# The second layer's output projection as three half-precision products, with VectorE writing the low half of the turned y

## What is computed

```python
    y = jnp.einsum('bhqk,bkhd->bqhd', att, v)
    y = y.reshape(Bx, Tx, HD)
    return y @ w_out
...
x = x + _L1_attn_ref(xn, w_kv_down, w_kv_up, w_q, w_out) + _L1_ffn_ref(xn, ...)
```

## Time and profile before

| | |
|---|---|
| median of 3 runs | 2831.82 us |
| the profiled execution: its own time, its span | 2835.03 us, 2833.2 us |
| PE, matmul busy | 2749.2 us, 97% of the span, 28612 instructions |
| DVE busy | 2341.8 us, 83%, 4378 instructions |
| ACT busy | 2078.8 us, 73% |
| POOL (GpSimd) busy | 1556.0 us, 55% |
| mean granted TensorE clock | 0.994 of full speed |

### The profile page before, as it was taken

How to read it: one execution, slowest core, us unless ns; L and a number is a source line. 1 busy time by engine, 2 the same in 40 slices (tenths; PEclk the granted TensorE clock), 3 DMA queues, 4 the chain that set the end, 5 groups by cost and what they waited for, 6 DMA issues and landing times.

```text
span 2833.2 us, 74040 instructions
## 1 busy us (share of the span) xinstructions
PE 2749.2 (97%) x28612; PEld 1665.3 (59%) x28612; DVE 2341.8 (83%) x4378; ACT 2078.8 (73%) x4411; POOL 1556.0 (55%) x1360
## 2 busy tenths in 40 slices
PE   5999999999999997999999999999999999999999
PEld 3656666666556553655665655656556656655665
DVE  6888888888888768988888888888888888888886
ACT  3777777777777776777777777777767767767766
POOL 2333343343333334766666666657656666666665
PEclk8999999999999998999999999999999999999999
DMA  4222222222222225344353444444444443443442
GB/s 136 58 57 68 75 65 64 58 64 64 57 58 68 69 71 158 95 113 110 86 128 96 99 119 107 99 109 114 102 109 105 102 114 91 110 118 84 108 119 52
DMA packets 249052, 260.52 MB, mean 92 GB/s; under 512 B 28288, under 2 KB 228992, under 8 KB 248448
## 3 DMA queue, kind: packets, MB, share of 16 engines
q1 hardware_dynamic: 226000, 239.70, 33.5%
q10 hardware_dynamic: 22704, 16.09, 1.9%
HBM read 107.84 MB, written 21.50 MB: 46 GB/s over the span
## 4 chain that ended last, share of the span: by engine, by line
PE 54%; DVE 5%; SPq 1%; issue 1%; DMA 1%; ACT 0%; DVEq 0%
PE l_ps_any L1584 7%; PE l_ps_any L1585 7%; PE l_ps_any L1586 7%; PE l_ps_any L1720 6%; PE l_ps_exp L1679 4%; PE l_ps_exp L1681 4%; PE l_ps_any L1729 4%; PE l_ps_any L1578 3%; PE l_ps_any L1654 3%; PE l_ps_out L1701 2%; PE l_ps_out L1704 2%; DVE l_neg_max L1512 2%; PE l_ps_out L1702 2%; PE l_ps_exp L1683 2%; SPq L1221 1%; DVE l_hw L1542 1%
## 5 line engine op out<-in xcount | busy, mean ns | idle before, releaser
L1278 POOL TENSOR_TENSOR stage<-l_p_in,stage 128x512 f16<-128x512 f32 x640 | 768.3, 1216 | 360.7 <-ACT l_p_in L1389 360.7
L725 DVE TENSOR_REDUCE neg_max<-ps_any 128x1 f32<-128x384 f32 (+3 forms) x704 | 407.1, 636 | 96.4 <-PE ps_any L854 92.8
L1287 POOL TENSOR_TENSOR l_hid<-l_hid,l_spread 128x512 f32<-128x512 f32 x256 | 347.6, 1358 | 215.8 <-DVE l_hid L1538 150.2
L1385 ACT ACTIVATE stage<-l_ps_exp 128x512 f16<-128x512 f32 x640 | 386.3, 604 | 91.5 <-PE l_ps_exp L1683 85.2
L477 POOL TENSOR_SCALAR_AFFINE_SELECT probs<-probs 128x512 f32<-128x512 f32 x256 | 162.1, 648 | 454.6 <-ACT probs L569 406.1
L569 ACT ACTIVATE probs<-ps_exp 128x512 f32<-128x512 f32 x640 | 348.3, 600 | 65.1 <-PE ps_exp L869 60.4
L1389 ACT ACTIVATE l_p_in<-l_ps_exp 128x512 f32<-128x512 f32 x640 | 388.7, 607 | 0.0
L1512 DVE TENSOR_REDUCE l_neg_max<-l_ps_any 128x2 f32<-128x768 f32 (+2 forms) x384 | 314.3, 859 | 16.0 <-PE l_ps_any L1659 15.8
L1679 PE MATMUL l_ps_exp<-l_q_a,l_k_a 128*128 128x512 f16 (+3 forms) x1024 | 303.4, 299 | 1.0 <-DMA l_q_b<-l_max_row 1.0
L1681 PE MATMUL l_ps_exp<-l_q_b,l_k_b 66*128 66x512 f16 (+3 forms) x1024 | 295.5, 300 | 0.0
L1542 DVE TENSOR_TENSOR l_hw<-l_hid,l_hw 128x512 f16<-128x512 f32 x272 | 260.6, 958 | 36.9 <-ACT l_hw L1367 36.5
(11 more groups left out here) (270 smaller groups left out, 7282.5 us busy)
## 6 DMA issues: line engine op xcount, KB each, us to landing
l_spread<-route_scratch SPq DMA_DIRECT2D x128, 512.0 KB, 4.4
l_q_a<-l_q_hi SPq DMA_DIRECT2D x256, 128.0 KB, 2.4
l_q_b<-l_q_lo SPq DMA_DIRECT2D x128, 128.0 KB, 2.4
l_k_a<-l_k_hi SPq DMA_DIRECT2D x128, 128.0 KB, 2.4
l_k_a<-l_k_lo SPq DMA_DIRECT2D x128, 128.0 KB, 2.4
l_k_b<-l_k_hi SPq DMA_DIRECT2D x128, 128.0 KB, 2.5
q_st<-rot_hi SPq DMA_DIRECT2D x64, 128.0 KB
k_st<-rot_hi SPq DMA_DIRECT2D x64, 128.0 KB
```

The lines of the kernel that those rows point to most:

```text
L725: nc.vector.tensor_reduce(neg_max[:, n % 2, heads[0]:heads[0] + k, t], src, AX.X, ALU.max, negate=True).then_inc(drained["dve"], 1)
L1278: nc.gpsimd.tensor_tensor(probs[:, n % 2, 1, u], p_in[:, m % P_SLOTS], probs[:, n % 2, 0, u], ALU.subtract).then_inc(p_lo_ok.sem, 1)
L1287: nc.gpsimd.tensor_tensor(at, at, spread[:, c % 3, n % SPREAD], ALU.mult).then_inc(weighted.sem, 1)
L1385: nc.scalar.activation(probs[:, n % 2, 0, u], bank, ACT.Exp, scale=float(HD1) ** -0.5).then_inc(exp_done.sem, 1)
```

## The change

`out` becomes three f16 products of halves. `yT` holds two halves in f16 in the same bytes. ACT writes the high half, without scale; DVE writes the low half with `low_part`, and it is now DVE's read that empties the bank of `turn_y`. `w_out` is loaded to `acc`'s space and halved once, with `w_d`. The scale is taken out when `out` is added to `acc`, in one instruction as before.

```diff
-        w_out = sb("w_out", [P, PAIRS, D])
+        w_out = sb("w_out", [P, 2, PAIRS, D], F16)
...
-        yT = sb("yT", [P, PAIRS, T])
+        yT = sb("yT", [P, PAIRS, 2, T], F16)
...
+        w_out_in = acc[:].rearrange("p s (k d) -> p (s k) d", d=D)
...
-        banks = Banks(program, filled_by1, filled_by1, lambda step: step[0] in ("gate", "cT", "turn_max", "turn_y"))
+        banks = Banks(program, filled_by1, filled_by1, lambda step: step[0] in ("gate", "cT", "turn_max"))
...
-        late_loads.append([(w_out[:], a["L1_attn_w_out"].rearrange("(k p) d -> p k d", p=P))])
+        late_loads.append([(w_out_in, a["L1_attn_w_out"].rearrange("(k p) d -> p k d", p=P))])
...
-        split_late = [(w_u, w_u_in), (w_d, w_d_in)]
+        split_late = [(w_u, w_u_in), (w_d, w_d_in), (w_out, w_out_in)]
...
                     act.wait_ge(down_loaded, 32)
+                    act.wait_ge(out_loaded, 16)
                     high_weights(split_late[1:])
...
-                    nc.scalar.activation(yT[:, n], bank, ACT.Copy, scale=1.0 / V_SCALE).then_inc(drained["act"], 1)
+                    nc.scalar.activation(yT[:, n, 0], bank, ACT.Copy).then_inc(y_hi_ok.sem, 1)
...
+                if name == "turn_y":
+                    if b and n % SET == 0:
+                        filling(dve, f"out{b - 1}_{n // SET}")
+                    low_part(f"turn_y{b}_{n}", yT[:, n, 1], yT[:, n, 0], 1.0, y_hi_ok, y_hi_ok.at(PAIRS * b + n, 1))
...
-                    nc.vector.tensor_tensor(acc[:, b % 2], full(dve, f"out{b}_{n}"), acc[:, b % 2], ALU.add
-                                            ).then_inc(drained["dve"], 1)
+                    nc.vector.scalar_tensor_tensor(out=acc[:, b % 2], in0=full(dve, f"out{b}_{n}"),
+                                                   scalar=1.0 / (W_SCALE * V_SCALE), in1=acc[:, b % 2], op0=ALU.mult,
+                                                   op1=ALU.add).then_inc(drained["dve"], 1)
...
                     for p in range(SET * n, SET * n + SET):
-                        ins = pe.matmul(out, w_out[:, p], yT[:, p], start=(p == SET * n), stop=(p == SET * n + SET - 1))
+                        for cw, cy in ((0, 0), (0, 1), (1, 0)):
+                            ins = pe.matmul(out, w_out[:, cw, p], yT[:, p, cy], start=(p == SET * n and cw + cy == 0),
+                                            stop=(p == SET * n + SET - 1 and cw == 1))
```

More of the change, by code:

```diff
@@ L1129, in layer1 @@
         w_u_in = experts_of_all(hw[:].rearrange("p s c t -> p (s c t)").bitcast(F32))
-        w_d_in = experts_of_all(yT[:].rearrange("p n t -> p (n t)"))
+        w_d_in = experts_of_all(yT[:].rearrange("p n c t -> p (n c t)").bitcast(F32))
+        w_out_in = acc[:].rearrange("p s (k d) -> p (s k) d", d=D)
         program = layer1_program(batches)
-        banks = Banks(program, filled_by1, filled_by1, lambda step: step[0] in ("gate", "cT", "turn_max", "turn_y"))
+        banks = Banks(program, filled_by1, filled_by1, lambda step: step[0] in ("gate", "cT", "turn_max"))
         up_loaded, down_loaded, out_loaded, weights_hi, weights_lo, prep, prep_pool = [
@@ L1165, in layer1 @@
         weighted = sig("weighted", 1)
+        y_hi_ok = sig("y_hi_ok", 1)
         hw_hi = sig("hw_hi", 1)
@@ L1724, in _ @@
                     if b == 0:
-                        pe.wait_ge(out_loaded, 16)
+                        pe.wait_ge(weights_lo, len(split_in) + len(split_late))
                     emptied(pe, f"turn_y{b}_{SET * n + SET - 1}")
```

## The result

| | before | after |
|---|---|---|
| median | 2831.39 us (4 runs, 2828.69 to 2832.66) | 2891.41 us (4 runs, 2890.30 to 2893.79) |
| the profiled execution: its own time, its span | 2835.03, 2833.2 us | 2892.00, 2889.9 us |

The ratio is 1.021, with a 95% interval of 1.0198 to 1.0222: 60 us slower. The forecast was 37 us slower, 2868.5 in 2843 to 2890. The side was right; the size was not, and the time lies just past the range. The clock (0.993) is as before.

The account below looks back on a forecast made before the run. PE's stream sets the pace, but only a few fills ahead of DVE's bank emptying; places 36.6 us, halving `w_out` +1.2, tail -1.1 gave +36.7 on 2835.03: 2871.7, less 3.2 for the median, 2868.5, range 2843 to 2890.

Parts of the forecast that it names:

- the leads at the banks: Second layer: an added 0.60 us DVE pass costs what PE's lead at that bank lacks; busy shares don't decide.
- PE's part: At a turn's two `out` steps, f16 products save 0.85 and 0.94 us; after waits 0.04 and 0.03 remain.
- `turn_y` 0, 1, 4, 7: Low halves there, per turn: 0 costs 0.53 us, 1 nothing; 4 and 7 leave gains of 0.04 and 0.03.
- `turn_y` 2: Low half there makes PE stand 1.23 us for its bank; part comes back, 0.5 a turn taken.
- `turn_y` 5 and 6: Low halves there make PE's fourth `max` of the group 1.14 us late, the price of both per turn.
- `turn_y` 3: Low half delays the routing 2.33 us; idle pieces on DVE leave PE's first `max` 0.27 late a turn.
- The range: Forecast's own 2839 to 2889 us, from 0.4 to 3.6 a turn; cut at the low end: 2843 to 2890.
- (a): Rival: PE's stream is the bound, DVE's additions fall in its 14.5% idle time; 28 us less, 2804; chance 0.07.
- (b): Rival: PE's gains at the two `out` places and prices elsewhere cancel, 2826 to 2838 us; chance 0.07.
- (c): Rival: DVE is the bound throughout, each of eight passes adds 0.60 us, 4.8 a turn: 2909; chance 0.10.
- The rule that (a) names: Skill's advice to optimise the engine with the highest occupancy first, read as naming PE (99% against DVE's 85%).
- Signs: Expected after: PE waits several us a turn, ACT's `out` waits about 2.1 each, turn 2.4 longer, DVE near 88% busy.

Follow-up runs that it names:

- Experiments 3 to 9: Changed kernel with low halves or ACT copies moved, nine y slots, or two POOL passes shortened: singly 2869.81 to 2878.78 us, all moves together 2822.14 us.
- experiment 1: Changed kernel, but ACT's copy empties the `turn_y` bank again and DVE writes no low half (left out of the result): 2806.83 us, ratio 0.9907.
- experiment 6: Changed kernel with DVE's low half of `turn_y` 5 moved behind `norm_y` 7: 2876.52 us, ratio 1.0161.
- experiment 9: Changed kernel with low halves of `turn_y` 3, 0, 2, 5, 7 moved, ACT's copies of 2 and 7 sooner, nine y slots: 2822.14 us, ratio 0.9963.

## Why the prediction missed

- **That the leads at the banks decide, and not the shares.** Right: slower with PE at 99% and DVE at 85%. Experiments 3 to 9 move 69 us without taking away a pass.
- **PE's part, 28 us at most, next to nothing kept.** Right: -0.4 in the table for both places against -1.1. Alone it is worth 27 (experiment 1).
- **`turn_y` 0, 1, 4, 7.** Right within 1.5 us each. At `turn_y` 4 the wait stands at both `max` steps as worked out.
- **`turn_y` 2.** Right: 1.22 a turn is paid and half comes back, 9.4 against 8.0. That the size fits is in part luck, for the 0.5 was chosen between 0.3 and 1.23 and not worked out.
- **`turn_y` 5 and 6.** 18.7 against 17.1. The mechanism was right but not the place: half of the delay shows already at the second `max`, where I had looked only at the fourth. The 1.4 at the last `turn_y` 7 is theirs as well; it goes in experiment 6.
- **`turn_y` 3: the step that failed.** "DVE ... starts the routing at 2149.67 instead of 2147.34, 2.33 late" came true (2.34: 1.27 after ACT's copy starts, instead of 1.07 ahead of it). The error is in what follows, "It has idle pieces behind that ..., so L1538 starts at 2155.88": this moves the routing as a block of fixed length. It took 4.63 instead of 3.64, so `l_k_lo` started 3.32 late and not 2.33. Of its 3.64 before, 0.58 was a wait already, to be read in a row of 0.81 among rows of 0.23; that wait has a length only relative to POOL. 19.6 us instead of 4.1.
- **The range.** Its upper end let each place cost DVE's whole lateness as I had worked it out, with no allowance for lateness growing. The terms as measured, 55 us, stand within 2 us of that end; with 3.0 not placed and 3 between this execution and the medians' difference, the result is past it.
- **Rivals.** (a) is out, its time is that of experiment 1. (b) is out. (c) is out by experiment 9 and by DVE's 13.5% of idle time. The rule that (a) names is given there in half: the same section of the Trainium skill ("Perfetto Trace Analysis", section Identifying the Most-Contended Engine) judges TensorE by the busy share of its weight loads and its floating-point throughput, and not by matmul busy time. Weight loads were busy 59%, less than DVE, so the rule doesn't plainly name PE here.
- **Signs.** The waits for the low half and L1515, ACT's 2.0 and the places came as written; the turn is 4.1 longer in the rows (3.9 on average) and not 2.4; DVE is at 86.5% in the stretch shown, 87.2% from 1180 to 2700, and not near 88, for PE's standing stretched the turn that DVE's work is divided by.

## What to carry to other kernels

Where results pass through a few banks in a fixed order, price an added pass at each place by the lead of the engine that wants the bank, and look for a place where the pass is due late and its operand there: here the places were worth 69 us, while the passes at the better places cost 16 (experiment 9 against 1). A pass that needs another engine's output can cost its queue that wait as well, so add when its operand is ready to the price of a place (`turn_y` 3 and 5: 62 us of waits). When an instruction is shifted in time, its duration in the trace may not go with it: if rows of one shape differ in length, find what the long ones end with before moving them.

## What the runs showed of the hardware

- The routing's `l_keep` and `l_weight` (128x64, both inputs in SBUF) ended 0.07 to 0.08 us after the POOL pass that was running, and took 0.23 to 0.28 instead of 0.70 to 1.21 when it was short. The wider `l_hw` (128x512, both inputs in SBUF) ended 0.55 after the POOL pass in which it started (median of 239 in the kernel before). `l_k_lo` and the low halves of y, which read PSUM, took 0.67 to 0.69 throughout.
- Three f16 products of 512 columns against one in f32: 2.59 us for four pairs of heads at `out` 1, as the sum had it, and 2.76 at `out` 0, instead of 3.4 to 3.5.
- Delays on separate places nearly add up: single moves 77.3 us, together 69.3.
